# Two decoder layers in one program: how the engines meet between stages, and when semaphores are cleared

## The reference, cut to what matters

```python
# x (4, 512, 512); ctx_2048 (4, 1601, 512); D = 512, 16 heads of 32, FF = 2048
x = x + cross_attention_0(layernorm(x), ctx_2048)   # q and projection on values quantised to int8 steps
x = x + ffn_0(layernorm(x))                         # W2 @ gelu(0.1 * clip(round(W1 @ h / 0.1)))
x = x + cross_attention_1(layernorm(x), ctx_2048, mask)  # scores clipped to +-50; result scaled, normed, gamma, beta
x = x + ffn_1(layernorm(x))                         # relu MLP plus an expert weighted by top-2 routing
```

## Time and profile before

| | |
|---|---|
| time, median of 3 | 2679.82 us (2678.22 to 2679.88) |
| the profiled execution | 2677.74 us, span 2676.0 us |
| TensorE busy | 2535.9 us, 95% of the span |
| VectorE | 1800.8 us, 67% |
| GpSimd | 1292.7 us, 48% |
| ScalarE | 1239.5 us, 46% |
| instructions | 34010 |
| TensorE's mean granted clock | 0.983 of full |

### The profile page before, as it was taken

The page is one execution under the profiler, slowest core; times in us unless marked ns, Lnnn a source line. Parts: engine busy times, 40 slices in busy tenths (PEclk is TensorE's granted clock), DMA queues, the critical chain, the costliest instruction groups (busy, mean ns, idle before and its releaser), DMA issues. The chain is left out here.

```text
span 2676.0 us, 34010 instructions
## 1 busy us (share of the span) xinstructions
PE 2535.9 (95%) x13272; PEld 1636.4 (61%) x13272; DVE 1800.8 (67%) x2488; ACT 1239.5 (46%) x1869; POOL 1292.7 (48%) x337
## 2 busy tenths in 40 slices
PE   8999999998999999999998999998899999997998
PEld 8888888986445454454535777786433333334776
DVE  5554544555777677777764666654699999997774
ACT  3222221312666666666662222222688888883211
POOL 0000000002999999999980000000599999995310
PEclk9999999998999999999999999999899999998999
DMA  8677666665353453534406644434987777774200
GB/s 299 232 239 254 233 248 248 200 194 143 77 118 78 87 109 66 116 80 85 109 5 216 219 145 164 144 132 128 205 183 164 164 164 163 165 208 130 80 32 32
DMA packets 218434, 405.11 MB, mean 151 GB/s; under 512 B 18169, under 2 KB 93977, under 8 KB 218209
## 3 DMA queue, kind: packets, MB, share of 16 engines
q1 hardware_dynamic: 218272, 402.93, 54.5%
HBM read 260.63 MB, written 140.59 MB: 150 GB/s over the span
## 5 line engine op out<-in xcount | busy, mean ns | idle before, releaser
L1371 POOL TENSOR_TENSOR pooled<-pooled,probs 128x2048 f32<-128x2048 f32 x140 | 640.9, 4578 | 20.1
L1218 ACT ACTIVATE probs<-psum 128x512 f32<-128x512 f32 (+1 forms) x832 | 458.5, 598 | 343.6 <-PE psum L1109 338.8
L1245 DVE TENSOR_REDUCE win_max<-psum 128x1 f32<-128x802 f32 x480 | 455.2, 988 | 151.3 <-PE psum L1074 151.1
L2053 DVE TENSOR_SCALAR probs<-psum,bound 128x1024 f32<-128x1024 f32 (+1 forms) x416 | 498.8, 1275 | 29.8 <-POOL pooled L2079 23.9
L2020 ACT ACTIVATE probs<-probs 128x1024 f32<-128x1024 f32 (+1 forms) x416 | 437.3, 1058 | 81.0 <-DVE probs L2053 38.7
L2079 POOL TENSOR_TENSOR pooled<-pooled,probs 128x2048 f32<-128x2048 f32 x94 | 433.2, 4609 | 13.1 <-ACT probs L2020 0.2
L1109 PE MATMUL psum<-q_st,k_st 128*128 128x512 f32 (+1 forms) x832 | 334.3, 438 | 18.4 <-ACT probs L1218 12.2
L253 POOL TENSOR_TENSOR r_q<-ve_q,minus_half 128x4 f32<-128x4 f32 x8 | 9.1, 1133 | 668.6 <-DVE ve_q L213 668.6
L1109 PEld LDWEIGHTS psum<-q_st,k_st 128*128 128x128 f32 (+1 forms) x832 | 149.0, 185 | 240.9 <-ACT probs L1218 179.4
L1074 PE MATMUL psum<-k_st,q_st 96*128 96x402 f32 x960 | 266.6, 359 | 6.2 <-DVE o_sb L1276 5.2
L1966 PE MATMUL psum<-q_st,k_st 128*128 128x512 f32 (+1 forms) x832 | 253.0, 430 | 17.9 <-DVE probs L2053 8.7
(11 more groups left out here) (258 smaller groups left out, 4267.9 us busy)
## 6 DMA issues: line engine op xcount, KB each, us to landing
k_st<-k_hi SPq DMA_DIRECT2D x64, 801.0 KB, 12.0
k_st<-k_lo SPq DMA_DIRECT2D x48, 801.0 KB, 11.2
k_hi<-kt_hi SPq DMA_DIRECT2D x32, 801.0 KB, 4.3
k_lo<-kt_lo SPq DMA_DIRECT2D x32, 801.0 KB, 6.0
v_rows<-v_out SPq DMA_DIRECT2D x96, 256.0 KB
v_st<-v_rows SPq DMA_DIRECT2D x24, 768.0 KB
q_st<-q_hi SPq DMA_DIRECT2D x64, 256.0 KB, 10.8
w<-w_hi_d SPq DMA_DIRECT2D x64, 256.0 KB, 3.1
```

The source lines that it names most:

```text
L1218: A.activation(probs[i % NPROBS][0:rows, j, :], bank(score_banks.where["score", u, t, j])[0:rows, :], ACT.Exp, scale=1.0 / ROOT).then_inc( ...
L1245: V.tensor_reduce(win_max[:, r, j, c:c + 1], window(windows.where["max", u, i])[:, :, 0:MV], AX.XY, ALU.max).then_inc(max_done, 1)
L1371: G.tensor_tensor(pooled[u % 2][:], before[:], probs[tile(u, k) % NPROBS][:], ALU.add).then_inc(pool_added, 1)
L2053: V.tensor_scalar(probs[i % NPROBS][0:rows, half * W:half * W + W, :], window(("score", u, t, half))[0:rows], bound[0:rows, u // NG, t:t + 1],
```

## The change

`close()` keeps only the first meeting. The stage's semaphores are put on a list `retired` and stay allocated; `clear_retired()` lets SyncE clear and free them later: those of stage 1 in stage 2 after the first unit's loads, those of stage 2 in stage 3 after the first 18 loads, those of stage 3 in stage 4 at u = 2, and those of stages 4 and 5 after stage 5's `close()`, followed by the meeting that ends the program. Each stage's semaphores get names of their own.

Three waits move from the end of a stage into the next one. `v_stored` is awaited by SyncE in stage 2 after `load_v(0)` and `load_v(1)`; stage 2's `o_stored` in stage 3 after the first weight loads; `p_stored` in stage 4 by SyncE at u = 1 and by VectorE ahead of its third tile.

```diff
-        def opened(scope):
-            mine = []
+        retired = []
+        def opened(stage):
+            mine, held = [], ExitStack()
             def sem(name):
-                mine.append(scope.enter_context(nc.semaphore(name)))
+                mine.append(held.enter_context(nc.semaphore(f"{stage}_{name}")))
                 return mine[-1]
             def close():
                 nc.all_engine_barrier()
+                retired.append((mine, held))
+            return sem, close
+        def clear_retired():
+            for mine, held in retired:
                 for s in mine:
                     Y.sem_clear(s)
-                nc.all_engine_barrier()
-            return sem, close
+                held.close()
+            retired.clear()
...
# kv_and_q_projection, end of sp_program; returns v_stored
-                    for s in range(NV):
-                        Y.wait_ge(v_stored[s], 16 * len(range(s, B * 2 * TT, NV)))
...
# attention_0, sp_program
                     load_v(0)
                     load_v(1)
+                    for s, v in enumerate(v_stored):
+                        Y.wait_ge(v, 16 * len(range(s, B * 2 * TT, len(v_stored))))
                     for s in (1, 2):
                         load(k_st[s][96:128, :, :], k_st[0][96:128, :, :], rows_set)
                     for u in range(UNITS):
+                        if u == 1:
+                            clear_retired()
...
                     store_o(UNITS - 1)
-                    Y.wait_ge(o_stored, 16 * UNITS)
...
# ffn_0_and_q_projection_1, sp_program (all_stored is attention_0's o_stored)
                         load_w1(f)
                         if f < NW2:
                             load_w2(f)
+                    Y.wait_ge(all_stored, 16 * UNITS)
+                    clear_retired()
                     beside = halves()
...
                     Y.wait_ge(stored, 16 * B)
-                    for i in range(2):
-                        Y.wait_ge(p_stored[i], 32 * UNITS // 2)
                     Y.wait_ge(early_landed, 16 * 10)
...
# attention_1, dve_program, clip
                         rows, i = TROWS[t], tile(u, t)
+                        if i == 2 and half == 0:
+                            for p in p_stored:
+                                V.wait_ge(p, 32 * UNITS // 2)
...
# attention_1, sp_program
                     load_v(1)
                     for u in range(UNITS):
+                        if u == 1:
+                            for p in p_stored:
+                                Y.wait_ge(p, 32 * UNITS // 2)
+                        if u == 2:
+                            Y.wait_ge(scored, score(1, 0, 0))
+                            clear_retired()
                         if u + 1 < UNITS:
...
# out_projection_and_ffn_1, end
                 close()
+                clear_retired()
+                nc.all_engine_barrier()
```

More of the change, by code:

```diff
@@ L347, in kv_and_q_projection @@
                 sbuf = allocator(scope)
-                sem, close = opened(scope)
+                sem, close = opened("a")
                 TILES = 2 * (NG * len(KCH) + TT)
@@ L979, in kv_and_q_projection, with attention_0 @@
                 close()
-        def attention_0(next_k, next_q, win_max, first):
+                return v_stored
+        def attention_0(next_k, next_q, win_max, first, v_stored):
             NQ, NSLOT, NPROBS, LAG, CLOSE_AT, TURN_AT, WINDOWS = 3, 3, 8, 2, 4, 11, 3
@@ L988, in attention_0 @@
                 sbuf = allocator(scope)
-                sem, close = opened(scope)
+                sem, close = opened("b")
                 k_st = [*next_k, sbuf("k_st02", [P, HPG, TP], F32R)]
@@ L1424, in attention_0, with ffn_0_and_q_projection_1 @@
                 close()
-        def ffn_0_and_q_projection_1(first, early_k, x_hi, x_lo, v_view, mask_i, bound):
+                return o_stored
+        def ffn_0_and_q_projection_1(first, all_stored, early_k, x_hi, x_lo, v_view, mask_i, bound):
             with ExitStack() as scope:
                 sbuf = allocator(scope)
-                sem, close = opened(scope)
+                sem, close = opened("c")
                 NW2, IN_KEYS = 4, HPG * TP // D
@@ L1878, in ffn_0_and_q_projection_1 @@
                 close()
+                return p_stored
         def advance(side, pieces):
@@ L1882, in advance, with attention_1 @@
                 next(side, None)
-        def attention_1(k_st, q_st, early_v, bound, cols, acc_sb, den_sb, last):
+        def attention_1(k_st, q_st, early_v, bound, cols, acc_sb, den_sb, p_stored, last):
             n, NQ, NSLOT = 1, 4, 3
@@ L1897, in attention_1 @@
                 sbuf = allocator(scope)
-                sem, close = opened(scope)
+                sem, close = opened("e")
                 v_st = [early_v, sbuf(f"v_st{n}1", [P, TT, P])]
@@ L2527, in build @@
             win_max = sbuf("win_max", [P, RT, HPG, 2])
-            kv_and_q_projection(context, rows, next_k, next_q, win_max)
-            attention_0(next_k, next_q, win_max, first)
+            v_stored = kv_and_q_projection(context, rows, next_k, next_q, win_max)
+            o_stored = attention_0(next_k, next_q, win_max, first, v_stored)
         with ExitStack() as scope:
@@ L2536, in build @@
             mask_i, bound = sbuf("mask_i", [P, B, TT], I32), sbuf("bound", [P, B, TT])
-            ffn_0_and_q_projection_1(first, early_k, early_q, early_v, v_view, mask_i, bound)
+            p_stored = ffn_0_and_q_projection_1(first, o_stored, early_k, early_q, early_v, v_view, mask_i, bound)
             handover.close()
@@ L2544, in build @@
             bo, gamma, beta = sbuf("o1_bo", [P, D]), sbuf("o1_gamma", [P, D]), sbuf("o1_beta", [P, D])
-            last_sem, last_close = opened(scope)
+            last_sem, last_close = opened("f")
             w_landed = {name: last_sem(f"{name}_landed") for name in ("wo", "wu", "wd", "we")}
@@ L2575, in build @@
             last = Last(sbuf, last_sem, last_rows, ahead())
-            attention_1(k_st, q_st, v_view, bound, cols, acc_sb, den_sb, last)
+            attention_1(k_st, q_st, v_view, bound, cols, acc_sb, den_sb, p_stored, last)
             spare = [*(third(k_st[0], i) for i in range(3)), q_st[0][:]]
```

## The result

The changed kernel takes 2662.35 us (median of 4, 2660.04 to 2664.92), the kernel before, measured beside it, 2679.02 (median of 4, 2676.15 to 2679.88). The ratio is 0.994, with a 95% interval of 0.9923 to 0.9957: 16.7 us faster, more than the 0.2% that can be told from no change. The range of 2661 to 2671 us holds it; the forecast of 2665.6 was 3.3 us too high, and the median lies nearer the 2661.7 of the first rival, so it is the trace that has to tell the two apart. The profiled execution lasted 2661.79 us, span 2659.9.

The account below looks back on a forecast made before the run. Idle stage ends, where no engine works, were taken to set the time one for one: 4.65 + 4.2 + 5.3 + 1.45 - 1.4 = 14.2 us off, giving 2665.6 us against the median, range 2661 to 2671.

Parts of the forecast that it names:

- the first rival: TensorE resumes at 2.4 GHz at the second, third and fourth stages' starts: 3.9 us less, 2661.7 us; chance 0.14.
- The SyncE drain: Second and third stage ends: SyncE's drain behind its last store issue takes 0.47 us, as at the fourth.
- the 2.1 us: Step from profile to median: the profiled execution of the kernel before lay 2.1 us below its median of 2679.82.
- The clears in the stages: SyncE's queue in stages two to four: 54, 36 and 63 clears take 3.1, 2.5 and 3.6 us, delaying nothing needed.
- Cost 0: Third stage: cols, issued 2.5 us later, finds the same backlog of weight loads; cost 0, upper bound 2.5 us.
- The clock: TensorE's clock still falls in the shorter gaps at three stage starts; net effect taken as 0, kept +2.5 and -3.9.
- as feared: Third stage: a later clock fall would lie on its first matmuls and could cost 1.5 to 2.9 us.
- the zero: Net effect of TensorE's clock at the three stage starts, taken as 0 us.
- The clock that stays up: TensorE at 2.4 GHz at all three starts, worth at most 3.9 us: 2661.7 us; chance 0.14.
- The first meeting that stays: SyncE's drain or another wait holds the first meeting until stores land; only 9.85 us gained, 2670.0 us; chance 0.08.
- Stages that give it back: A stage's start or course is bound by a transfer not coming earlier; within 5.4 us remains, 2676 us; chance 0.05.
- Dearer clears beside a full queue: Third stage: clears ahead of cols stretch to 0.9 us each, 15.7 us slower, 2695 us; chance 0.03.

Follow-up runs that it names:

- cols sooner: Changed kernel with one clear per run of consecutive semaphores, plus the third stage's cols load moved ahead of the last 6 weight loads: 2654.09 us, 0.9911.
- clears behind cols: Changed kernel with the third stage's 36 clears issued four times over, just behind the load of cols: 2662.38 us, 0.9941.
- cheap clears in before: Kernel before, with close() clearing each run of neighbouring semaphores by one instruction; both meetings and all waits stay: 2665.07 us, 0.9955.
- waits alone: Changed kernel with the waits for the last stores put back at the first three stage ends, clears still spread: 2667.56 us, 0.9963.
- changed, again: The changed kernel measured once more with no edit: 2661.26 us, 0.9939.
- kept busy: Changed kernel with clears by ranges, plus 60 unread identity matmuls on TensorE around the first three meetings: 2660.45 us, 0.993.
- ranges: Changed kernel with one clear per run of consecutive semaphores, in the stages and in the tail: 2658.0 us, 0.9927.
- ranges, again: Later repeat of the changed kernel with one clear per run of consecutive semaphores, as yardstick: 2657.93 us, 0.9923.
- four times: Changed kernel with the third stage's 36 clears issued four times over, ahead of the load of cols: 2669.05 us, 0.9966.
- clears ahead of the loads: Changed kernel with the moved waits and clears ahead of the next stage's first loads (fourth stage's p_stored clears stay at u = 2): 2665.43 us, 0.9955.

## Why the prediction was right, and by how much it was off

What sets the time, the order at the stage ends, and the direction were right. End by end, in us, each as the stretch from the work that comes last to the release, before less after:

| end | forecast | measured | from |
|---|---|---|---|
| 1 | 4.65 | 4.7 | VectorE's drain end: (641.9 - 637.05) - (636.1 - 635.95) |
| 2 | 4.2 | 4.6 | last issue: (1419.9 - 1415.01) - (1408.9 - 1408.60) |
| 3 | 5.3 | 5.7 | last issue: (1894.9 - 1888.82) - (1879.3 - 1878.95) |
| 4 | 1.45 | 1.4 | SyncE's drain end: (2433.9 - 2432.3) - (2416.4 - 2416.2) |
| 5 | -1.4 | -1.3 | first to last meeting: (2675.9 - 2672.4) - (2659.9 - 2655.1) |
| sum | 14.2 | 15.1 | |

**The SyncE drain** is the term that was mis-sized: "a SyncE drain just behind an issue took 0.47 us at the fourth end", taken over to the second and third. It is 124 and 7 ns there: 0.8 us in all. That the last thing late at the first end is VectorE's drain was right, and that the fourth end keeps its 466 ns.

**The rest** of the 16.1 us between the spans, 1.0, is in no meeting. The first stage's VectorE work ended 1.1 us earlier with nothing changed in it, and the others differ by +0.6, -1.1, +0.5 and -0.2. The two large ones are falls of the clock: the kernel before has one near 573 us that the changed one lacks, and the changed one has the one near 1543 us, 134 us into the third stage, that the kernel before lacks at that place. Against the median, the 2.1 us that were added to the profiled execution's time were 1.3 once a fourth execution of the kernel before had moved its median, and 0.6 for the changed one. These make up the 3.3 us: 0.9 in the ends, 0.8 outside them, 1.5 in the step from profile to median (2.1 - 0.6), with rounding.

**The clears in the stages** cost what was said, 3.0, 2.4 and 3.6 us of SyncE's time, and nothing else. The load of cols is issued 11.2 us after the release instead of 9.1 and takes 7.5 us to land instead of 9.7: the backlog was there, and VectorE starts on cols 18.7 us after the release, before 18.9. But this cover was all there was. The two runs with clears ahead of and behind cols show that beyond it the time goes with the load: a start on cols 4.4 us later than the changed kernel's for a stage 4.9 to 6.5 us longer, falls of the clock included. And the load was already what held the stage, as the run with cols sooner shows. "Cost 0" was right for this size alone.

**The clock** fell at all three starts, as said; the one at the third came later and lay on the first matmuls, as feared: 0.50 from 1410 to 1416.5 us, ScalarE's first work on the first code tile 10.7 us after the release for 9.6. It cost nothing that can be seen: across the versions the third stage's length doesn't go with that moment (9.7 us after the release with a length of 469.5, 11.8 with 466.9), but with the moment at which VectorE starts on cols and with the falls of the clock some 134 us into the stage. In us, all twelve profiles:

| start on cols, after the release | length without that fall | length with it |
|---|---|---|
| 16.2 | 465.1 (cols sooner) | |
| 17.9 | 466.6 (clears behind cols) | |
| 18.1 | | 467.8 (cheap clears in before), 467.5 (waits alone) |
| 18.7 | 466.9 (changed, again) | 468.5 (changed) |
| 18.8 | | 469.5 (kept busy; fall twice as long) |
| 18.9 | 467.4 (before), 467.1 (ranges) | |
| 19.3 | | 468.8 (ranges, again) |
| 23.1 | | 473.4 (four times; one more fall) |
| 23.3 | 471.9 (clears ahead of the loads) | |

With 1.7 us taken off for each fall, all twelve lie within 1 us of one line on which a start 1 us later is a stage some 0.9 us longer; that slope is an estimate from these rows. TensorE's lost time at the start and its idle time behind f_g_lo (1.85 + 1.08 us before, 0.49 + 1.08 after) trade against each other. So the zero was right to about 1 us, with a better reason than the one given. The Trainium skill (TensorE: Matmul & The Clock Gate, Why this matters for your kernels) speaks against long idle gaps between bursts; in the trace gaps of 2.0 and 2.9 us with thin work around them already brought the low level. The execution in which it was kept away shows that this is worth at most about 1 us in the third stage and less in the others, and the added work held the meetings by 1.2 us.

**The rivals.** The clock that stays up falls by the trace, and its 3.9 us by the run that forced it. The first meeting that stays falls: SyncE's drain is over in 7 to 466 ns with stores under way. By the Trainium skill (PSUM — Partial Sum Buffer, Engine vs sequencer instructions) a drain waits for its engine to be idle; the rows show that transfers which SyncE has issued are no part of that. Stages that give it back: middles unchanged. Dearer clears beside a full queue: 62 ns.

What stays open: why the clock falls behind one and the same gap in some executions and not in others, how many falls the executions without a profile had, and so where the 1.8 us lie by which the waits are dearer in the medians than in the trace, and why three executions of the run kept busy were slower. A version with ranges, cols sooner and a clock kept up wasn't tried.

## What to carry to other kernels

Count the instructions between two meetings before moving them: a clear costs its 57 to 69 ns each, one over a range costs 0.06 to 0.13 us for all, and that simpler edit alone gained 12.5 us where the change gained 16.8. A wait for a last store belongs where the data is read or the semaphore cleared, not ahead of a meeting. When work is moved onto a queue, look for the one load behind it that an engine already waits for: put the work behind that load, or the load ahead (23.8 us under the kernel before together with the ranges, the fastest version here, for 16.8 of the change). And before two single profiles are compared for a gain of 1 or 2 us, compare the granted clock behind the waits in the middle of the stages: one fall more or less was 1.7 us here.

## What the runs showed that I had not expected

SyncE's drain took 7 ns behind the stores of the first and the third end, 124 ns behind the o_sb store, and 466 ns behind the last den_d store, the same at that end in every version; I don't know what sets it apart. A clear of a range took 125 ns for 54 semaphores, 86 for 36, 132 for 63 and 59 for 22. And the third stage's first transfers cover a load of cols that is issued 2.0 us later to within 0.2 us, while one issued 8.6 us later (17.7 us after the release for 9.1) came out as a start 4.2 us later.
